# New order tables for a hand-ordered pipeline of four graph layers

## The reference

```
x = layernorm(x + Z),  Z from 4 hops z = 0.9 * P z + 0.1 * v,  P = softmax(mask(q k^T)), 8 heads     # layer 0
x = layernorm(x + softmax(mask(x G x^T)) x V O + bo)                                                   # layer 1
x = layernorm(x + softmax(mask(q k^T)) v Wo + bo), 8 heads                                             # layer 2
agg_d = sum over neighbours with label d of x Wd_d, over their number;  out = relu(sum_d agg_d + bd)
r, z = sigmoid(out W + x W);  n = tanh(out Wni + r * (x Wnh));  x = layernorm((1 - z) n + z x)          # layer 3
```

## Time and profile before

| what | value |
|---|---|
| three runs | 1592.68, 1594.06, 1594.12 us, median 1594.06 us |
| the profiled execution, its own time | 1598.14 us |
| its span, first to last instruction | 1596.3 us |
| PE busy | 1537.3 us, 96% |
| DVE busy | 1285.9 us, 81% |
| ACT busy | 1239.0 us, 78% |
| POOL busy | 700.1 us, 44% |
| granted clock of TensorE, mean | 0.991 |

### The profile page before, as it was taken

One profiled execution on the slowest core, in us unless ns is written; L12 is line 12 of the kernel. 1 busy time (PEld: TensorE's weight loads), 2 busy tenths in 40 slices (PEclk: granted clock), 3 DMA queues, 4 the chain that ended last, 5 costly groups with the idle time before them and its releaser, 6 DMA issues.

```text
span 1596.3 us, 44413 instructions
## 1 busy us (share of the span) xinstructions
PE 1537.3 (96%) x17268; PEld 1396.3 (87%) x17268; DVE 1285.9 (81%) x3164; ACT 1239.0 (78%) x4074; POOL 700.1 (44%) x710
## 2 busy tenths in 40 slices
PE   7888999999999999999999999999999999999996
PEld 6777998998999899989989999989989998998885
DVE  3676888888888888888888888888888888888775
ACT  4667877878887888888787888778788878888663
POOL 1244454344544444454444454443445444444422
PEclk7999999999999999999999999999999999999998
DMA  5101000111100110110011011001111001100000
GB/s 201 35 24 29 25 20 25 35 32 31 35 28 15 35 34 28 35 34 28 15 35 35 28 35 31 20 27 34 33 30 35 28 15 35 35 21 25 15 11 21
DMA packets 71426, 51.64 MB, mean 32 GB/s; under 512 B 4401, under 2 KB 69937, under 8 KB 70577
## 3 DMA queue, kind: packets, MB, share of 16 engines
q1 hardware_dynamic: 71216, 48.79, 10.0%
HBM read 40.39 MB, written 8.39 MB: 31 GB/s over the span
## 4 chain that ended last, share of the span: by engine, by line
PE 62%; ACT 33%; DVE 2%; issue 1%; DMA 1%; POOL 0%; SPq 0%; POOLq 0%; DVEq 0%; ACTq 0%
ACT E L797 10%; ACT E L861 8%; PE bank_B L488 6%; PE bank_B L718 6%; PE bank_A L532 6%; PE bank_C L488 5%; PE bank_A L488 5%; PE bank_B L532 4%; ACT PT L803 3%; PE bank_A L718 3%; PE bank_A L506 3%; PE bank_B L500 3%; PE bank_A L518 2%; PE bank_X L638 2%; PE bank_A L616 2%; PE bank_B L526 2%
## 5 line engine op out<-in xcount | busy, mean ns | idle before, releaser
L942 POOL TENSOR_TENSOR E<-E,rsum 128x512 f32<-128x512 f32 x256 | 270.6, 1057 | 477.3 <-DVE rsum L1135 322.0
L950 POOL TENSOR_TENSOR rstd<-var,minus_half 128x2 f32<-128x2 f32 x128 | 94.2, 745 | 388.8 <-DVE var L1088 388.8
L803 ACT ACTIVATE PT<-bank_C 128x512 f32<-128x512 f32 x128 | 87.0, 680 | 64.2 <-PE bank_C L526 64.2
L1096 DVE TENSOR_SCALAR y<-y,mv,rstd 128x256 f32<-128x256 f32 x192 | 91.0, 516 | 25.8 <-POOL rstd L950 25.7
L1036 DVE COPY_PREDICATED_SCALAR bank_A<-absent,fill 128x512 f32 x128 | 92.3, 743 | 15.2 <-PE bank_B L518 14.4
L488 PE MATMUL bank_A<-xT_hi,w_hi 128*128 128x256 f32 x376 | 97.6, 284 | 0.0
L861 ACT ACTIVATE E<-bank_A,nmax 128x128 f32<-128x128 f32 x256 | 93.0, 408 | 3.9 <-DVE nmax L1131 3.9
L488 PE MATMUL bank_A<-xT_hi,w_lo 128*128 128x256 f32 x376 | 94.9, 277 | 0.0
L797 ACT ACTIVATE E<-bank_B,nmax 128x128 f32<-128x128 f32 x256 | 94.9, 443 | 0.0
L1036 DVE COPY_PREDICATED_SCALAR bank_B<-absent,fill 128x512 f32 x128 | 94.8, 741 | 0.0
L861 ACT ACTIVATE E<-bank_B,nmax 128x128 f32<-128x128 f32 x256 | 92.3, 403 | 1.8 <-DVE nmax L1131 1.8
(11 more groups left out here) (298 smaller groups left out, 6306.4 us busy)
## 6 DMA issues: line engine op xcount, KB each, us to landing
xt_in<-in_xt SPq DMA_DIRECT2D x64, 128.0 KB, 2.3
absent<-in_adj SPq DMA_DIRECT2D x64, 128.0 KB, 2.8
x_in<-in_x SPq DMA_DIRECT2D x32, 256.0 KB, 3.1
out<-y SPq DMA_DIRECT2D x31, 256.0 KB, 2.1
adj<-in_adj SPq DMA_DIRECT2D x32, 128.0 KB, 3.3
adjT<-in_adjt SPq DMA_DIRECT2D x32, 128.0 KB, 3.1
stage<-in_weights SPq DMA_DIRECT2D x3, 1024.0 KB, 10.7
row<-in_rows SPq DMA_DIRECT2D x1, 1024.0 KB, 8.0
```

The source lines that it names most:

```text
L803: nc.scalar.activation(PT0[:, part].rearrange("p g c n -> p (g c n)"), C0[:, :], ACT.Copy, scale=1.0 - ALPHA).then_inc(pt0_ready.sem, 1)
L942: nc.gpsimd.tensor_tensor(e, e, rs[:, part].unsqueeze(2).to_broadcast([P, SB, P]), ALU.mult).then_inc(e_sig.sem, 1)
L950: nc.gpsimd.tensor_tensor(rstd[part][:], var[part][:], minus_half[:], ALU.pow)\
L1096: a = nc.vector.tensor_scalar(to[:, g, :], src[g], mv[part][:, g, 0:1], rstd[part][:, g:g + 1], ALU.subtract, ALU.mult)
```

## The change

Only the two tables are new; no step is added or taken away, and the code that carries the steps out is the same (its line numbers are 12 higher). Of each engine's list the order and the lags differ. The core of the diff:

```diff
 ORDER = {
     "tensor": [
-        "n3@4 k0 wo2.0@3 wo2.1@3 hop0.6@1 hop0.7@1 n2@2 back0.6@1 back0.7@1 q0 lab.0@4 lab.1@4 k2@2 q2@2 v2@2 agg.0@4",
...
+        "hop0.5@1 hop2.0@3 hop2.1@3 back0.4@1 k0 back0.5@1 n3@4 wo2.0@3 wo2.1@3 hop0.6@1 hop0.7@1 n2@2 back0.6@1",
...
     "scalar": [
-        "exp2.0@3 exp0.0@1 g1@2 lab.3@5 exp2.1@3 exp0.1@1 acc.1@5 p0.0@1 vo1@2 p0.1@1 out@5 nh@5 exp0.2@1 exp1@2 r@5",
...
+        "exp2.1@4 exp0.1@2 acc.1@6 vo1@3 p0.0@2 x0@1 wtb@5 out@6 exp0.2@2 nh@6 p0.1@2 exp1@3 r@6 exp0.3@2 p0.2@2 p1@3",
...
     "gpsimd": [
-        "pow.3@5 absent.0 absent.2@2 pow.1@2 pow.0@1 pow.2@3 sc.3@5",
+        "ne1@1 e2.2@3 e2.3@3 pow.3@5 absent.2@2 pow.1@2 sc.3@5 absent.0 sc.1@2 pow.0@1 sc.0@1 e2.0@2 sh.3@5 e0.0",
...
     "sync": [
-        "ldw.0 ldw.1@4 ld_adj.2@3 ld_x@2 ld_adj.0@1 ld_adj.1@2 ld_adj.3@4 ld_xt store@6",
+        "ldw.0@2 ld_x@1 ld_adj.3@3 ld_xt ld_adj.2@2 ld_adj.1@1 ld_adj.0 ldw.1@2 store@6",
     ],
 }
```

More of the change, by code:

```diff
@@ L61 @@
     "tensor": [
[4 rows of a table removed]
[4 rows of a table added]
     ],
     "scalar": [
[5 rows of a table removed]
[5 rows of a table added]
     ],
     "gpsimd": [
-        "sh.3@6 sc.1@3 sc.0@2 e2.0@3 e0.0@1 sh.0@2 ne1@2 e0.1@1 sh.1@3 e2.1@3 e0.2@1 e1@2 e0.3@1 e2.2@3 e2.3@3",
-        "pow.3@5 absent.0 absent.2@2 pow.1@2 pow.0@1 pow.2@3 sc.3@5",
+        "ne1@1 e2.2@3 e2.3@3 pow.3@5 absent.2@2 pow.1@2 sc.3@5 absent.0 sc.1@2 pow.0@1 sc.0@1 e2.0@2 sh.3@5 e0.0",
+        "e2.1@2 e0.1 sh.1@2 sh.0@1 e0.2 e1@1 pow.2@3 e0.3",
     ],
     "vector": [
[7 rows of a table removed]
[8 rows of a table added]
     ],
     "sync": [
-        "ldw.0 ldw.1@4 ld_adj.2@3 ld_x@2 ld_adj.0@1 ld_adj.1@2 ld_adj.3@4 ld_xt store@6",
+        "ldw.0@2 ld_x@1 ld_adj.3@3 ld_xt ld_adj.2@2 ld_adj.1@1 ld_adj.0 ldw.1@2 store@6",
     ],
@@ L96 @@
     "tensor": [
[6 rows of a table removed]
[7 rows of a table added]
     ],
     "scalar": [
[8 rows of a table removed]
[13 rows of a table added]
     ],
     "gpsimd": [
[4 rows of a table removed]
+        "e2.2@2 absent.2@1 e2.3@2 pow.3@4 ne1 sc.3@4 pow.1@1 pow sc sc.1@1 e2@1 sh.1@1 pow.2@2 sh.3@4 e1 e2.1@1 sh",
+        "e2.2@1 absent.2 e2.3@1 pow.3@3 pow.1 sc.1 pow.2@1 e2 e2.1 sc.3@3 sh.3@3 e2.2 e2.3 pow.3@2 sh.1 pow.2 pow.3@1",
+        "sc.3@2 sh.3@2 sc.3@1 sh.3@1 pow.3 sc.3 sh.3",
     ],
     "vector": [
[14 rows of a table removed]
[19 rows of a table added]
+        "o_lo nrm.3@1 gate sum mixa mixb mixc bn.3 agg.3 eps.3 nrm.3",
     ],
     "sync": [
-        "ld_adj.2@2 ld_x@1 ld_adj.1@1 ld_adj.3@3 ld_adj ld_adj.1 ld_adj.3@2 ld_adj.2@1 store@5 ld_x ld_adj.2 store@4",
-        "ld_adj.3@1 ld_adj.3 store@3 store@2 store@1 store",
+        "ld_adj.1 store@5 ld_x ld_adj.3@2 ld_adj.2@1 ld_adj.3@1 store@4 ld_adj.2 ld_adj.3 store@3 store@2 store@1",
+        "store",
     ],
```

## The result

The changed kernel takes **1585.7 us** (median of four runs, 1584.7 to 1586.7), against 1594.1 for the kernel before, measured beside it: ratio 0.9942, 95% interval 0.9929 to 0.9955. That is 8.4 us faster. The forecast was 1568 us, with a range of 1556 to 1584: the sign is right and the size is not. The profiled execution took 1585.51 us, span 1583.7, so against the profile before (1598.14) it is 12.6 us less, where the prediction's sum said 26.

The account below looks back on a forecast made before the run. TensorE's own work was taken as the bound, with only its idle time and overlap to win. Steady 15 + start 9 + end 2 = 26 us less than the profiled 1598.1, or 1568 us against the median; range 1556 to 1584.

Parts of the forecast that it names:

- rival B: Only the start is won, since a new wait replaces each old one in the steady cycle: 1585 us, chance 0.13.
- Start, `ldw.0`, 5.4 us: Pair 1's `xt_in` goes out ahead of group 5's load, ending ScalarE's `x0` wait and TensorE's idle time: 5.4 us together.
- Start, the large splits, -0.4 on VectorE: `split.3` and `split.4` on VectorE go into the 4.25 us hole ahead of pair 1's `back0.0`; 0.4 us given back.
- Start, `p2.0`, 4.2 us: In pairs 2 and 3 `p0.3` no longer stands behind the waiting `p2.0`: 2.7 and 1.5 us, 4.2 together.
- Start, `split.2`, 0.9 us: Pair 0's `k0` copy no longer stands behind a split waiting for weights; all of pair 0 moves up by 0.9 us.
- Steady, the three waits, 0.75 us: TensorE's waits ahead of `s1`, `s02.1` and `hop0.0` shrink or go: 0.33 + 0.2 + 0.22 = 0.75 us per period.
- s1 swap: ScalarE copies `vnat1` ahead of `PT0`, so TensorE's wait ahead of `s1` goes: 0.33 us per period.
- `max2.0` swap: VectorE finishes `max2.0` before `fill0.0`, so `exp0.1` ends sooner for `s02.1`: 0.2 us per period.
- `hop0.0` term: `p2.0` leaves the place ahead of `p0.3`, so the wait ahead of `hop0.0` shrinks to some 0.05: 0.22 us per period.
- Steady, what stands against it, 0.2 us: GpSimd's `ne1` collides with VectorE's `mixb`, making `back0.0`, `hop0.2` and `mixt` late: 0.2 us lost per period.
- End, 2 us: In the tail `z` of pair 30 moves ahead of pair 31's `n3` and waits are dealt anew: 2 us, bounds -4 and +7.

Follow-up runs that it names:

- e3: The kernel before with only the change's load order on SyncE (group 5's load behind pair 1's `xt_in` and `x_in`); ratio 0.9967 to the kernel before.
- e1: The changed kernel with ScalarE's `x0` moved back behind `p0.3`, ahead of `hop0.0`; ratio 0.9909 to the kernel before.
- e2: The changed kernel with `split.3` and `split.4` put back in their old places on VectorE; ratio 0.992 to the kernel before.
- e7: The changed kernel with one swap on VectorE, `v0` ahead of `rec2.1`; ratio 0.9918 to the kernel before.
- e6: The kernel before with one ScalarE swap in the steady order, the `vnat1` copy (`vo1`) ahead of the `PT0` copy (`p0.0`); ratio 0.9967 to the kernel before.
- e11: The changed kernel with one VectorE swap undone in the steady order, `fill0.0` ahead of `max2.0` again; ratio 1.0015 to the kernel before.
- e12: The kernel of e11 with `v0` also ahead of `rec2.1` on VectorE; 1599.46 us in one run.

## Why the prediction was wrong

The sum was 9 + 15 + 2 = 26 us; in the two profiles it is 4.2 + 8.7 - 0.2, 12.6 unrounded. Part of that is chance of the profile before: pair 0 took 1.8 us less when profiled again. Drops of the clock weigh on both sides: 1.5 us in pair 2 before, 1.1 in pair 1 and 1.4 in the tail of the change. The medians differ by 8.4, and the interval reaches to 11.3. The time of rival B came out, but not its mechanism.

- *Start, `ldw.0`, 5.4 us.* **This step failed first.** The price was right (6.1 us of pair 0 alone, e3). What failed is the half sentence "lands with the first loads, before ScalarE reaches `x0`". The prediction took the landing from the place in the queue and `x0`'s turn from the kernel before, though the same change moves `x0` ahead of `exp0.2`. It costs 5.0 us (e1).
- *Start, the large splits, -0.4 on VectorE.* **Failed.** The hole of 4.25 us ahead of `back0.0` held them, but GpSimd had `e0.3` to do in it, and TensorE waited for that. It costs 1.8 us, and 2.9 where the clock drops behind the wait, as in the change's profile (e2, e7). The prediction had the row that prices this, an `e2.2` of 3.00 us beside a split, and the Trainium skill's rule (SBUF — State Buffer, "Who interferes with whom"); it used both for `mixb` and `ne1` and not for the splits it moved itself. The trace agrees with the rule: 3.00 for 1.04 us beside the split.
- *Start, `p2.0`, 4.2 us.* The sum came out: pairs 2 and 3 gained 2.3 and 1.6 us. But in pair 2 the prediction took `p0.3` at 105.27, behind a `p2.0` and 8 fillers at half clock, and priced all of that as order. e3 and e6 have the old order at full clock and take 39.5 us, so the order is worth 0.7 there and the clock 1.5. In pair 3, at full clock on both sides, it is 1.6 for 1.5. No run had `p2.0` alone.
- *Start, `split.2`, 0.9 us.* Its mechanism is seen: `kT` is copied at 8.05 instead of 9.14. No run had it alone.
- *Steady, the three waits, 0.75 us.* Right in place and nearly in size: 0.66. The overlap of 0.16 us was read where transposes follow aggregation matmuls; ahead of `s02.1`, `s1` and `hop0.0` it is 0.07. So the ceiling was 0.44 + 3 x 0.07 = 0.65, not 0.92. Singly the terms were less well sized: the s1 swap is worth 0.18 alone (e6) for 0.33, the `max2.0` swap 0.52 in this order (e11) for 0.2. Such terms are not independent; e12, where the wait only moves on to `exp0.1`, points to the one run of exponentials that they share. The `hop0.0` term had no run of its own.
- *Steady, what stands against it, 0.2 us.* The wrong thing was priced. The collision came (`mixa`, beside `e2.2`, takes 1.09 us in the median, for 0.68 before), but `hop0.2` and `mixt` did not come later for it. **What was left out** are `g1` waiting for `lo1` and `p0.0` for `v0`, 0.26 us, and 0.10 for neighbours and matmul rate, which the prediction put at 0 ("TensorE's sum stays"). Both come with the order: the `max2.0` swap itself makes `lo1` 0.13 us later (e11 takes that back), and `v0` stands behind `rec2.1` (e7).
- *End, 2 us.* **Failed**, inside its bounds. The idle time was dealt anew and none of it went. Some 1.2 us are won by it where the clock stays up (e7), and in the change's profile the clock behind the new wait of 3.04 us takes them back.
